# Attention scores as three float32r products, modulation rows on four partitions, and a reordered first head

## The reference, cut to what matters

```python
mod = (_silu(L0_c) @ L0_wmod).reshape(L0_c.shape[0], 6, 1, -1)
sa, ca, ga, sb, cb, gb = (mod[:, 0], mod[:, 1], mod[:, 2], mod[:, 3], mod[:, 4], mod[:, 5])
ga = (2 * (ga >= 0) - 1) * jnp.maximum(jnp.abs(ga), 0.25)
h = _layernorm(x, axis=-1) * (1 + ca) + sa
...
scores = jnp.einsum('bhtd,bhsd->bhts', q, k) * scale
scores = LOGIT_SOFTCAP * jnp.tanh(scores / LOGIT_SOFTCAP)
scores = jnp.where(mask[None, None], -jnp.inf, scores)
attn = jax.nn.softmax(scores, axis=-1)
out = jnp.einsum('bhts,bhsd->bhtd', attn, v)
```

## Time and profile before

| what | value |
|---|---|
| median of 3 runs | 1105.91 us (1103.24 to 1106.88) |
| profiled execution, its own time | 1108.44 us |
| span of the profiled execution | 1106.6 us |
| PE busy | 1028.6 us, 93% |
| PEld busy | 852.1 us, 77% |
| DVE busy | 612.9 us, 55% |
| ACT busy | 496.7 us, 45% |
| POOL busy | 408.3 us, 37% |

### The profile page before, as it was taken

One profiled execution on the slowest core, in us unless ns is written; L12 is line 12 of the kernel. 1 busy time (PEld: TensorE's weight loads), 2 busy tenths in 40 slices (PEclk: granted clock), 3 DMA queues, 4 the chain that ended last, 5 costly groups with the idle time before them and its releaser, 6 DMA issues.

```text
span 1106.6 us, 17331 instructions
## 1 busy us (share of the span) xinstructions
PE 1028.6 (93%) x5813; PEld 852.1 (77%) x5813; DVE 612.9 (55%) x1424; ACT 496.7 (45%) x909; POOL 408.3 (37%) x598
## 2 busy tenths in 40 slices
PE   3999999999999999999999999999989788888884
PEld 3689989889989989998988998998754555455452
DVE  3575455658567765766776666676367221112116
ACT  1355555555555555555455555555430033333330
POOL 2132222223223555322465432235516244444450
PEclk9999999999999999999999999999999899999985
DMA  9970000000000101100011012000021199999957
GB/s 355 346 258 0 0 0 1 1 1 24 16 1 13 55 36 43 39 1 1 24 42 37 21 39 84 1 10 23 3 100 42 39 246 258 250 241 260 264 92 227
DMA packets 59583, 96.70 MB, mean 87 GB/s; under 512 B 8091, under 2 KB 41638, under 8 KB 59008
## 3 DMA queue, kind: packets, MB, share of 16 engines
q1 hardware_dynamic: 41440, 74.78, 20.8%
q0 software_dynamic: 11808, 14.16, 6.2%
q10 hardware_dynamic: 6272, 6.93, 2.3%
HBM read 63.21 MB, written 40.67 MB: 94 GB/s over the span
## 4 chain that ended last, share of the span: by engine, by line
PE 72%; DMA 13%; DVE 7%; issue 4%; POOL 1%; another core or an unknown queue 1%; ACT 1%; POOLq 0%; ACTq 0%; SPq 0%; DVEq 0%
PE ps L1196 24%; PE ps L1243 13%; PE ps L1219 12%; DMA acc<-wos,arena 12%; PE ps L1232 10%; PE ps L1205 2%; PE ps L1226 2%; PE ps L1208 2%; PE ps L1409 1%; PE ps L1424 1%; PE ps L1280 1%; PE ps L1355 1%; PE ps L1177 1%; PE ps L1260 1%
## 5 line engine op out<-in xcount | busy, mean ns | idle before, releaser
L411 POOL TENSOR_TENSOR holdp<-neghalf 128x1 f32<-128x1 f32 x145 | 31.5, 217 | 493.6 <-DVE ss L798 280.5
L566 ACT ACTIVATE prob<-ps,rn 128x512 f32<-128x512 f32 (+3 forms) x256 | 120.9, 525 | 150.6 <-PE ps L1219 150.1
L1196 PE MATMUL ps<-wh,hth 128*128 128x384 f32 x512 | 177.2, 346 | 6.2 <-DVE wl L752 6.2
L798 DVE TENSOR_REDUCE ss<-arena 128x8 f32<-128x1024 f32 x64 | 78.1, 1221 | 189.0 <-ACT arena L543 189.0
L1196 PE MATMUL ps<-wl,hth 128*128 128x384 f32 x512 | 171.9, 336 | 0.0
L1196 PE MATMUL ps<-wh,htl 128*128 128x384 f32 x512 | 171.8, 336 | 0.0
L543 ACT ACTIVATE arena<-ps 128x1024 f32<-128x1024 f32 x64 | 65.5, 1023 | 210.2 <-PE ps L1196 210.2
L1243 PEld LDWEIGHTS ps<-vx,prob 128*128 128x128 f32 x1280 | 152.9, 191 | 4.0 <-POOL prob L458 0.8
L1243 PE MATMUL ps<-vx,prob 128*128 128x129 f32 (+1 forms) x1280 | 153.4, 274 | 0.4 <-POOL prob L458 0.4
L1219 PE MATMUL ps<-qt,kt 128*128 128x512 f32 (+3 forms) x512 | 149.5, 435 | 1.8 <-DVE rows L792 1.6
L522 POOL DMA_INDIRECT acc<-wos,arena x64 | 90.2, 1409 | 118.6 <-DMA acc<-wos,arena 76.4
(11 more groups left out here) (172 smaller groups left out, 1575.7 us busy)
## 6 DMA issues: line engine op xcount, KB each, us to landing
wge<-in_wgu SPq DMA_DIRECT2D x32, 352.0 KB
slot_rows<-pay SPq DMA_DIRECT2D x1, 7728.0 KB, 35.0
arena<-slot_rows ACTq DMA_DIRECT2D x56, 120.8 KB
wde<-in_wd SPq DMA_DIRECT2D x32, 192.0 KB
prob<-in_wgu SPq DMA_DIRECT2D x16, 352.0 KB
arena<-in_wgu SPq DMA_DIRECT2D x16, 352.0 KB
warena<-in_wqkv SPq DMA_DIRECT2D x1, 4992.0 KB, 20.9
acc<-zrow SPq DMA_DIRECT2D x2, 2048.0 KB, 28.8
```

What stands on the lines that cost most here:

```text
L566: act_(prob[:, OFF[j]:OFF[j] + w], sflat[:, OFF[j]:OFF[j] + w], ACT.Tanh, scale=rn[:, bass.ds(head(n), 1), TT + j:TT + j + 1].squeeze(1)). ...
L798: nc.vector.tensor_reduce(ss[:].rearrange("p (c i) -> p i c", c=2), sq, X, ALU.add).then_inc(s["ss_rdy"], 1)
L1196: last = mm(ps[:, i, 0:3 * DH], hp[:, k, i * P:(i + 1) * P], wp[:, k, :], start=(k == 0 and m == 0), stop=(k == KC - 1 and m == 2))
```

## The change

It has three parts.

Scores. q and k of a head are each kept as two float32r tiles, a high part (`qth`, `kth`) and a low part (`qtl`, `ktl`), and each of the four score products becomes three float32r products accumulated in PSUM. ACT writes the high parts from PSUM (`qk_high`, between `out_t` and `exps`), and DVE writes the low parts as differences (`qk_t`).

Modulation rows. The four vectors are computed once for all batches, on four partitions (`ps[0:B, 6:8]`), clamped there on DVE, written to a DRAM tensor by SP and read back with a repeating transfer onto all 128 partitions (`rows_in`). The load of the modulation weights is split in two. The waits on SP stand behind its transfers that fill the tables.

First head. On DVE `ln_norm(0, 0)` no longer stands behind the loads of the small tensors and the columns' modulation, `weights_low(0, 0)` stands ahead of `h_modulated(0)`, and `h_high` and `h_low` go by halves. Two tiles of the expert stage move to another buffer.

```diff
--- before.py
+++ after.py
...
+        mod_d = nc.dram_tensor("mod_rows", (B, 4, D), F32, kind="Internal").ap()
...
-        qt = sb("qt", [P, T])
-        kt = sb("kt", [P, T])
+        qth = sb("qth", [P, T], F32R)
+        qtl = sb("qtl", [P, T], F32R)
+        kth = sb("kth", [P, T], F32R)
+        ktl = sb("ktl", [P, T], F32R)
...
-        scb = part(KC * B * P).rearrange("p (k b m) -> p k b m", k=KC, b=B)
-
-        rat = [at[0] - KC * 6 * D - KC * B * P]
+        mrow = part(4 * D)[0:B].rearrange("p (c d) -> p c d", c=4)
+        sign = part(2 * D)[0:B].rearrange("p (c d) -> p c d", c=2)
...
-        xgt = qt[:, 0:2 * KC * C].rearrange("p (u k c) -> p u k c", u=2, k=KC)
-        gact = kt[0:C, 0:2 * M].rearrange("p (u m) -> p u m", u=2)
+        xgt = h2s.rearrange("p k t -> p (k t)")[:, 0:2 * KC * C].rearrange("p (u k c) -> p u k c", u=2, k=KC)
+        gact = h2s.rearrange("p k t -> p (k t)")[0:C, 2 * KC * C:2 * KC * C + 2 * M].rearrange("p (u m) -> p u m", u=2)
...
-            sp.dma_start(wmods, wmod).then_inc(s["ld_wmod"], 16)
+            sp.dma_start(wmods[:, :, 0:2 * D], wmod[:, :, 0:2 * D]).then_inc(s["ld_wmod"], 16)
             sp.dma_start(wq[:, :, 0:nf, :], wqkv[:, :, 0:nf, :]).then_inc(s["ld_wq0"], 16)
+            sp.dma_start(wmods[:, :, 2 * D:6 * D], wmod[:, :, 2 * D:6 * D]).then_inc(s["ld_wmod2"], 16)
...
+            sp.wait_ge(s["mrow_rdy"], 1)
+            sp.dma_start(mod_d, mrow).then_inc(s["mrow_out"], 16)
+            sp.wait_ge(s["mrow_out"], 16)
+            sp.dma_start(rows[:].rearrange("p b c d -> p (b c d)"),
+                         mod_d.rearrange("b c d -> (b c d)").unsqueeze(0).to_broadcast([P, B * 4 * D])).then_inc(s["rows_in"], 16)
...
-            act_(modt[:].rearrange("p j b -> p (j b)"), ps[:, 0, 0:4 * B], ACT.Tanh).then_inc(s["modt_sb"], 1)
+            act_(modt[:].rearrange("p j b -> p (j b)"), ps[:, 2, 0:4 * B], ACT.Tanh).then_inc(s["modt_sb"], 1)
             a.wait_ge(s["modt_sb"], 1)
-            act_(modt[:].rearrange("p j b -> p (j b)"), ps[:, 0, 0:4 * B], ACT.Copy).then_inc(s["modt_sb"], 1)
...
-                a.wait_ge(s["h_full"], KC * (b + 1))
-                act_(hth[:], xn[:].rearrange("p i d -> p (i d)").rearrange("p (k t) -> p k t", k=KC), ACT.Copy).then_inc(s["h_high"], 1)
+                for k in range(KC):
+                    a.wait_ge(s["h_full"], KC * b + k + 1)
+                    act_(hth[:, k, :], xn[:].rearrange("p i d -> p (i d)").rearrange("p (k t) -> p k t", k=KC)[:, k, :], ACT.Copy).then_inc(s["h_high"], 1)
...
+            def qk_high(b, n):
+
+                if some(cnt(b, n - 1)):
+                    a.wait_ge(s["s_rdy"], 3 * cnt(b, n - 1))
+                a.wait_ge(s["qt_ps"], cnt(b, n))
+                act_(qth[:], ps[:, 2, :], ACT.Copy).then_inc(s["qth_rdy"], 1)
+                a.wait_ge(s["kt_ps"], cnt(b, n))
+                act_(kth[:], ps[:, 3, :], ACT.Copy, scale=g[:, bass.ds(head(n), 1)]).then_inc(s["kth_rdy"], 1)
...
+                if not (is_last(b) and static and p == H - 1):
+                    qk_high(b, p + 1)
...
+            a.wait_ge(s["g_rdy"], 4)
+            qk_high(0, 0)
             take(0, 1)
...
-                v.wait_ge(s["h_full"], KC * (b + 1))
-                v.wait_ge(s["h_high"], b + 1)
-                tt(htl[:], full, hth[:].bitcast(F32), ALU.subtract).then_inc(s["ht_rdy"], KC)
+                for k in range(KC):
+                    v.wait_ge(s["h_high"], KC * b + k + 1)
+                    tt(htl[:, k, :], full[:, k, :], hth[:, k, :].bitcast(F32), ALU.subtract).then_inc(s["ht_rdy"], 1)
...
-            for k in range(KC):
-                cp(scb[:, k], sc[:, k].unsqueeze(2).to_broadcast([P, B, P])).then_inc(s["scb_rdy"], 1)
-            def rows_out(b):
-
-                v.wait_ge(s["rows_ps"], b + 1)
-                bk = 4 + 2 * (b % 2)
-                cp(rows[:, b], ps[:, bk:bk + 2, :].rearrange("p a (u d) -> p (a u) d", d=D)).then_inc(s["rows_sb"], 1)
+            def rows_out():
+
+                v.wait_ge(s["rows_ps"], 1)
+                cp(mrow, ps[0:B, 6:8, :].rearrange("p a (u d) -> p (a u) d", d=D)).then_inc(s["rows_sb"], 1)
...
-                v.wait_ge(s["qt_ps"], cnt(b, n))
-                cp(qt[:], ps[:, 2, :]).then_inc(s["qt_rdy"], 1)
-                v.wait_ge(s["kt_ps"], cnt(b, n))
-                ts(kt[:], ps[:, 3, :], g[:, bass.ds(head(n), 1)], None, ALU.mult).then_inc(s["kt_rdy"], 1)
+                v.wait_ge(s["qth_rdy"], cnt(b, n))
+                tt(qtl[:], ps[:, 2, :], qth[:].bitcast(F32), ALU.subtract).then_inc(s["qt_rdy"], 1)
+                v.wait_ge(s["kth_rdy"], cnt(b, n))
+                nc.vector.scalar_tensor_tensor(out=ktl[:], in0=ps[:, 3, :], scalar=g[:, bass.ds(head(n), 1)], in1=kth[:].bitcast(F32),
+                                               op0=ALU.mult, op1=ALU.subtract).then_inc(s["kt_rdy"], 1)
...
-            def clamp_gate(n, c):
-
-                gate_rows = rows[:, :, c, :]
-                ts(sign, gate_rows, 0.0, 2.0, ALU.is_ge, ALU.mult).then_inc(s["clamp"], 1)
-                nc.vector.scalar_tensor_tensor(out=gate_rows, in0=gate_rows, scalar=-1.0, in1=gate_rows, op0=ALU.mult, op1=ALU.max).then_inc(s["clamp"], 1)
-                v.wait_ge(s["clamp"], 4 * n + 2)
-                ts(gate_rows, gate_rows, 0.25, None, ALU.max).then_inc(s["clamp"], 1)
-                v.wait_ge(s["clamp"], 4 * n + 3)
-                nc.vector.scalar_tensor_tensor(out=gate_rows, in0=sign, scalar=-1.0, in1=gate_rows, op0=ALU.add, op1=ALU.mult).then_inc(s["clamp"], 1)
-                v.wait_ge(s["clamp"], 4 * n + 4)
-
-            sign = w95[:].rearrange("p i e -> p (i e)").rearrange("p (b d) -> p b d", b=B)
+            def rows_signed():
+
+                v.wait_ge(s["rows_sb"], 1)
+                ts(mrow[:, 2, :], mrow[:, 2, :], 1.0, None, ALU.add).then_inc(s["clamp"], 1)
+                ts(sign, mrow[:, 0:4:3, :], 0.0, 2.0, ALU.is_ge, ALU.mult).then_inc(s["clamp"], 1)
+                nc.vector.scalar_tensor_tensor(out=mrow[:, 0:4:3, :], in0=mrow[:, 0:4:3, :], scalar=-1.0, in1=mrow[:, 0:4:3, :],
+                                               op0=ALU.mult, op1=ALU.max).then_inc(s["clamp"], 1)
+
+            def rows_clamped():
+
+                v.wait_ge(s["clamp"], 3)
+                ts(mrow[:, 0:4:3, :], mrow[:, 0:4:3, :], 0.25, None, ALU.max).then_inc(s["clamp"], 1)
+                v.wait_ge(s["clamp"], 4)
+                nc.vector.scalar_tensor_tensor(out=mrow[:, 0:4:3, :], in0=sign, scalar=-1.0, in1=mrow[:, 0:4:3, :],
+                                               op0=ALU.add, op1=ALU.mult).then_inc(s["mrow_rdy"], 1)
...
-                    if p == 0:
-                        v.wait_ge(s["rows_sb"], B)
-                        ts(rows[:, :, 2, :], rows[:, :, 2, :], 1.0, None, ALU.add).then_inc(s["cb_rdy"], 1)
-                    clamp_gate(p, (0, 3)[p])
+                    rows_signed() if p == 0 else rows_clamped()
...
+            ln_norm(0, 0)
+            v.wait_ge(s["modt_sb"], 2)
+            ts(modt[:, 2:4, :], modt[:, 2:4, :], 1.0, None, ALU.add).then_inc(s["modt_sb"], 1)
+            weights_low(0, 0)
+            v.wait_ge(s["modt_sb"], 3)
+            h_modulated(0)
+            h_low(0)
...
-            v.wait_ge(s["modt_sb"], 2)
-            ts(modt[:, 2:4, :], modt[:, 2:4, :], 1.0, None, ALU.add).then_inc(s["modt_sb"], 1)
             v.wait_ge(s["g_rdy"], 4)
-            v.wait_ge(s["modt_sb"], 3)
-            ln_norm(0, 0)
-            h_modulated(0)
-            h_low(0)
-            weights_low(0, 0)
+
             squares_sum(0, 0)
             q_scale(0, 0)
             weights_low(0, 1)
-            rows_out(0)
-            rows_out(1)
             qk_t(0, 0)
             squares_sum(0, 1)
+            rows_out()
             q_scale(0, 1)
             weights_low(0, 2)
-            rows_out(2)
...
-            v.wait_ge(s["cb_rdy"], 1)
+            v.wait_ge(s["rows_in"], 16)
...
-                    last = mm(ps[:, 0, j * B:(j + 1) * B], wmods[:, k, j * P:(j + 1) * P], sc[:, k, :], start=(k == 0), stop=(k == KC - 1))
+                    last = mm(ps[:, 2, j * B:(j + 1) * B], wmods[:, k, j * P:(j + 1) * P], sc[:, k, :], start=(k == 0), stop=(k == KC - 1))
             last.then_inc(s["modt_ps"], 1)
-            def mod_rows(b):
-
+            def mod_rows():
+
+                pe.wait_ge(s["ld_wmod2"], 16)
                 for h in range(2):
                     for k in range(KC):
-                        last = mm(ps[:, 4 + 2 * (b % 2) + h, :], scb[:, k, b, :], wmods[:, k, 2 * D + h * T:2 * D + (h + 1) * T],
+                        last = mm(ps[0:B, 6 + h, :], sc[:, k, :], wmods[:, k, 2 * D + h * T:2 * D + (h + 1) * T],
                                   start=(k == 0), stop=(k == KC - 1))
...
-                    last = mm(sflat[:, OFF[j]:OFF[j] + w], kt[:, j * P:(j + 1) * P], qt[:, T - w:T], start=True, stop=True)
+                    elif j == 2:
+                        pe.wait_ge(s["rows_sb"], 1)
```

(10 more changed lines are left out.)

9 lines of the change are left out of this document (5 added, 4 removed).

## The result

| | before | after |
|---|---|---|
| median | 1104.58 us (1101.18 to 1106.88, 4 runs) | 1084.53 us (1082.29 to 1088.81, 4 runs) |
| profiled execution, its own time | 1108.44 us | 1088.81 us |
| span of the profiled execution | 1106.6 us | 1087.0 us |
| scores of head 0 start | 48.31 us | 38.49 us |
| last head's scores start | 793.14 us | 775.54 us |

A forecast was written before the change was run, and what follows sets the result against it. PE's own work was taken to bound the attention stage, a chain between engines the start. The start's 12.6 us plus 15.5 from the periods gave 28.1 off 1105.9, so 1078 us, range 1069 to 1089.

The forecast's parts named there:

- its own case: Whole kernel: the forecast's main outcome, 1073 to 1083 us, given a chance of 0.60.
- the rivals that it put at 1083 and 1084: Narrow score products cost their weight load, 1083 us (chance 0.10); the start gains less, 1084 us (chance 0.10).
- For 128 columns I take 83 ns: Scores on PE: price of each 128-column float32r product, 83 ns, a third of 0.25 us for three products.
- the scores at 1.81 us: Scores on PE: twelve float32r products a head take 1.81 us, 0.35 less than before.
- The first rival, 1083 us: Scores on PE: narrow products cost their weight load, 110 ns each; a head gains 0.27, 1083 us; chance 0.10.
- The start, 12.6 us: Start of the kernel: `qkv` of head 3 starts at 50.1 instead of 62.69 us, 12.6 us gained.
- The transitions, 2.0 us each: Three batch transitions: delayed DVE work and shorter periods cost 2.0 us each, 6.0 in all.
- period 15 into head 0: Batch transition: `qkv` waits for the weights' low part while PE comes 0.35 us sooner; 0.4 us off.
- Steady part, 15.5 us: Attention periods behind the start: 62 heads at 0.35 us give 21.5, less 6.0 for transitions, 15.5 us gained.
- At no cost: DVE's clamping, SP's new waits, 2 MB more of rows to read and the expert tiles' new place cost nothing.
- The rival in which the operand chain becomes the bound: Attention periods: late low k stretches each period; slower if beyond 6.7 us, 1118 us at 6.9; chance 0.03.

The follow-up runs named there:

- e6_narrow_64: The changed kernel with 64 columns instead of 128 in the second and third pass of the narrowest score product; 1090.16 us (one run).
- e9_filled_both: The changed kernel with PE products that nothing reads in both gaps at the start; 1084.21 us, ratio 0.9840 to the kernel before.
- e4_dve_ahead: The changed kernel with DVE's late work of periods 1 and 12 ahead of q's and k's low parts; 1081.67 us, ratio 0.9805 to the kernel before.
- e5_high_first: The changed kernel with ACT's high parts ahead of the copy of the transposed output; 1090.39 us, ratio 0.9839 to the kernel before.

## Why the prediction was right, and where its sizes were off

Direction and range were right, and every mechanism named in the sum was there, but the sizes that were well off were all off to the same side. The measured 1084.5 us lies outside what the text calls its own case (1073 to 1083), near the rivals that it put at 1083 and 1084. It was close: 1105.9 less the 17.6 us found at the last scores is 1088.3, just inside the range that ends at 1089. The rest of the way to 1084.5 came with the stage behind, which was shorter by 2.0 us in the profiled run for no reason shown, and with the scatter of the medians; that part is luck. Two sizes made up most of the 10 us between the 28.1 forecast and the 17.6 found.

- **"For 128 columns I take 83 ns", the scores at 1.81 us.** This step failed. A product of 128 columns costs its weight load, 110 ns, and a head takes 1.92 us, so it gains 0.24 and not 0.35: 62 x 0.11 = 6.8 us. Of the 0.11 the load explains 3 x 0.027 = 0.08; the other 0.03 I did not take apart. The reading of the earlier trace rows was at fault: three products of 192, 128 and 64 columns in 0.25 us are not 83 each, because the product behind them pays. TensorE in order of time, the kernel before:

```profile
334.20 0.42 PE L1269 MATMUL ps<-selr,onesr 128*128 128x192 f32 x3
334.45 0.42 PE L1196 MATMUL ps<-wh,hth 128*128 128x384 f32 x1
334.71 0.34 PE L1196 MATMUL ps<-wl,hth 128*128 128x384 f32 x1
```

  The three take 0.25 between starts (334.20 to 334.45), but the product of 384 columns behind them then takes 0.26 instead of 0.17 (until 334.71), since the loads had kept their 0.11 and were 0.09 behind. The trace of before also had the price in the open, in its chain: the router's 16 products of 64 columns (`285.95 1.73 PE ps L1260 x16`), 0.11 us each, where I looked only at transposes. The first rival, 1083 us, had the mechanism, with 0.10 of the chance; it put 0.08 on a head. The Trainium skill (TensorE: Matmul & The Clock Gate, "LDWEIGHTS (loading the stationary operand)") gives a load its columns divided by 1.2 in ns, 107 ns for 128. The trace of `e6_narrow_64` agrees with it: the loads start 0.11 us apart.
- **The start, 12.6 us.** The first `qkv` (15.54), the gap of 5.4 us and the four-partition row products (3.53) came as forecast. That the weights' load would end together with the path through the modulation was not in the sum; it cost nothing, but a still smaller modulation load would have gained nothing either. Mis-sized was the low clock: the first `qkv` took 6.08 instead of 5.70, the transposes 1.96 instead of 1.8, and the second `qkv`, set at 5.0, took 5.96. That is 1.5 us, and the scores of head 0 took 2.11 instead of 1.81; the start gained 10.5. Single values vary: in runs with the same start the first `qkv` took 6.1 to 7.2 us and the second 4.7 to 6.1, but both together 11.4 to 12.5, always over the 10.7 forecast. That PE's standing still is the cause, as the text said, `e9_filled_both` shows.
- **The transitions, 2.0 us each.** About right. Against a gain of 0.24 in every period, the starts show 0.93 lost at period 12 (12.43 instead of 11.74; 0.95 forecast), 0.71 at period 1 (12.07 instead of 11.60; 0.65) and another 0.20 in the period behind it (11.60 instead of 11.64), 0.34 where the forecast says "period 15 into head 0" (0.4), and 0.17 behind period 10 (11.59 instead of 11.66) in the second to fourth batch, which was not foreseen. The 0.20 is no second stall but the rest of the wait at period 1: in the chain the scores behind a wait take 0.24 longer, and the sum left that out. That is 2.35 each, 7.1 in all instead of 6.0. `e4_dve_ahead` shows that DVE's order is the cause of what goes at period 12, about half, and of all at period 1; the rest of period 12 was not taken apart.
- **Steady part, 15.5 us.** Between `qkv` of head 3 and the last scores lie the scores of 61 heads. The rows show 7.1 us gained there (52.22 to 775.54, before 62.69 to 793.14): 61 x 0.234 = 14.3 less 7.1. With the start's 10.5 that is the 17.6; one head's 0.24 lies behind.
- **At no cost.** Held: no `qkv` waits for the copies in an ordinary period, low k ends 5.10 us into it (5.03 forecast), and the 2 MB of rows are issued at 76.6 us and read in 7.0, long before they are needed. The rival in which the operand chain becomes the bound fell; `e5_high_first` shows that 0.4 us more of slack changes no ordinary period.
- **What stays open.** The stage after the last scores differs by up to 11 us between runs whose code there is the same; the 2.0 us in which it was shorter after the change can't be told from that, and it was not taken apart.

## What to carry to other kernels

Price a chain of matmuls by the distance between starts, product by product, and take the larger of the streaming and the next weight load (here 110 ns for a load of 128 columns); a group's mean can hide it, because the product behind the group pays what is owed. Ask of a load that you make smaller what lands next: here the first heads' weights were due in the same 0.1 us. When PE gets faster, list the DVE work that is queued behind the copies in each special period first: three transitions took back 7 us of 14, and two moved steps returned 4.4. Work that moves out of the start may have been what covered a chain between engines and kept PE's clock up, so move it only with a replacement for both.
